# One shared-expert unit moved ahead of the block loop, routing of the last batches in other banks, and half of the last additions on GpSimd

## What is computed

```python
def reference(...):
    x = x + tanh(g_xattn[0]) * xattn(layernorm(x), ctx, ctx, mask, Wq, Wk, Wv, Wo, 16)
    h = layernorm(x)
    shared = (silu(h @ shared_gate.T) * (h @ shared_up.T)) @ shared_down.T
    probs = sigmoid(h @ router_w.T + routing_bias)
    scores, indices = top_k(probs, 2)            # scores divided by their sum
    g = silu(h @ gate_w[e]); u = h @ up_w[e]     # e: the two experts of the token
    combined = sum over the two of score * ((g * u) @ down_w[e])
    return x + tanh(g_ffn[0]) * (shared + combined)
```

## Time and profile before

| what | value |
|---|---|
| time, median of 3 runs | 181.72 us (181.02 to 184.23) |
| the profiled execution's own time | 181.07 us |
| its span, first to last instruction | 179.3 us |
| mean granted clock of PE | 0.993 of full |
| PE busy | 165.0 us, 92% |
| DVE busy | 126.9 us, 71% |
| POOL busy | 108.4 us, 60% |
| ACT busy | 109.3 us, 61% |

### The profile page before, as it was taken

One profiled execution on the slowest core, in us unless ns is written; L12 is line 12 of the kernel. 1 busy time (PEld: TensorE's weight loads), 2 busy tenths in 40 slices (PEclk: granted clock), 3 DMA queues, 4 the chain that ended last, 5 costly groups with the idle time before them and its releaser, 6 DMA issues.

```text
span 179.3 us, 4668 instructions
## 1 busy us (share of the span) xinstructions
PE 165.0 (92%) x1424; PEld 140.2 (78%) x1424; DVE 126.9 (71%) x613; ACT 109.3 (61%) x402; POOL 108.4 (60%) x137
## 2 busy tenths in 40 slices
PE   7899889999999999999999999988899999998960
PEld 7777669988889998779998779876586887886840
DVE  2779988756898766798776798778746666663364
ACT  3657997468588267598367698513546666663210
POOL 3666799846796816866706868686444666666200
PEclk9999999999999999999999999999999999999997
DMA  5999994900000000101000000013132222211063
GB/s 154 262 372 375 412 410 191 385 23 4 16 0 18 0 2 4 32 19 44 1 4 0 15 21 32 15 49 91 45 89 65 63 66 78 73 53 35 12 223 117
DMA packets 11095, 17.34 MB, mean 97 GB/s; under 512 B 2075, under 2 KB 6945, under 8 KB 10944
## 3 DMA queue, kind: packets, MB, share of 16 engines
q1 hardware_dynamic: 9504, 14.59, 24.0%
q0 software_dynamic: 1280, 2.20, 3.7%
q10 hardware_dynamic: 288, 0.26, 0.4%
HBM read 9.99 MB, written 7.51 MB: 98 GB/s over the span
## 4 chain that ended last, share of the span: by engine, by line
PE 62%; DVE 13%; ACT 8%; DMA 6%; POOL 5%; issue 4%; SPq 1%
PE misc L397 8%; PE pt L650 7%; PE s_even L360 6%; PE o_bank L386 6%; ACT probs L716 4%; PE pt L371 4%; PE proj_q L317 3%; DMA wq_raw<-wqT 3%; PE proj_k L317 3%; DVE probs L925 3%; PE proj_k L319 2%; PE pt L641 2%; PE proj_k L318 2%; PE proj_q L319 2%; PE proj_q L318 2%
## 5 line engine op out<-in xcount | busy, mean ns | idle before, releaser
L716 ACT ACTIVATE probs<-probs,negmax 128x128 f32<-128x128 f32 x128 | 50.0, 395 | 8.5 <-DVE negmax L925 8.5
L1311 POOL TENSOR_TENSOR probs<-probs,rinv 128x512 f32<-128x512 f32 x32 | 33.1, 1046 | 24.6 <-DVE rinv L939 24.3
L1420 POOL DMA_INDIRECT ys<-probsT,xg x23 | 22.5, 979 | 17.2 <-issue 10.7
L716 ACT ACTIVATION_READ_ACCUMULATOR probs<-probs,negmax 128x1 f32 x128 | 24.4, 191 | 0.0
L925 DVE CUSTOM_DVE_ANT_0 probs<-s_even,mask 128x128 f32<-128x128 f32 x64 | 18.1, 282 | 3.8 <-issue 3.8
L1341 POOL DMA_INDIRECT xs<-xrow,slot x16 | 16.3, 1019 | 6.5 <-issue 3.9
L371 PE MATMUL pt<-ident_sb,probs 128*128 128x128 f32 x128 | 17.6, 277 | 1.6 <-POOL probs L1311 1.1
L360 PE MATMUL s_odd<-kT,qT 64*128 64x128 f32 x128 | 18.5, 285 | 0.0
L360 PE MATMUL s_even<-kT,qT 64*128 64x128 f32 x128 | 18.5, 284 | 0.0
L925 DVE CUSTOM_DVE_ANT_0 probs<-s_odd,mask 128x128 f32<-128x128 f32 x64 | 18.1, 283 | 0.0
L650 PEld LDWEIGHTS pt<-down_sb,v 128*128 128x128 f32 x92 | 12.1, 190 | 7.2 <-issue 7.1
(11 more groups left out here) (279 smaller groups left out, 455.0 us busy)
## 6 DMA issues: line engine op xcount, KB each, us to landing
xs<-pad SPq DMA_DIRECT2D x5, 858.0 KB, 5.8
xg<-xs SPq DMA_DIRECT2D x23, 66.0 KB, 1.9
down_sb<-down SPq DMA_DIRECT2D x1, 1152.0 KB, 8.9
probs<-ys SPq DMA_DIRECT2D x4, 256.0 KB, 4.0
gu_raw<-gu SPq DMA_DIRECT2D x3, 256.0 KB, 6.5
wk_raw<-wkT SPq DMA_DIRECT2D x2, 256.0 KB, 3.8
wq_raw<-wqT SPq DMA_DIRECT2D x2, 256.0 KB, 5.0
mask<-mask SPq DMA_DIRECT2D x8, 64.0 KB, 2.0
```

The costliest lines, as they stand in the source:

```text
L716: e = act.activation(probs[:, r, l, :], probs[:, r, l, :], ACT.Exp, bias=negmax[:, r, l:l + 1], scale=-1.0, accum_out=rowsum[:, r, l:l + 1])
L1311: pool.tensor_tensor(quad, quad, rinv[:, r, 4 * u:4 * u + 4].unsqueeze(2).to_broadcast([P, 4, P]), ALU.mult).then_inc(norm_done, 1)
L1420: pool.indirect_dma_start(out=ys, out_offset=bass.IndirectOffsetOnAxis(ap=xg[n % IN_FLIGHT][:, P:P + 1].bitcast(U32), axis=0), in_=y_sb[n ...
```

## The change

Four things change. (1) PE works unit 0 of the shared expert ahead of the block loop, in place of the six fillers; unit 1 takes unit 0's place in the loop, and only units 2 and 3 are left behind it. ACT's and DVE's work on unit 0 moves to the first and second turn of the loop, that on unit 1 to the place where unit 0's was. (2) So that `proj_q` and `proj_k` are free for unit 0, routing rounds 3 and 4 (batches 6 and 7) use `pt0` and `pt1`. (3) POOL adds the first row of each pair into `x_sb`; DVE adds the second row after it, and the shared part last. (4) Pairs 0 and 1 are stored together once the first `add_shared` is done, pairs 2 and 3 together after the second. The banks of the units and of the down steps are renamed to match.

```diff
-        shared_banks = [(proj_bank["q"], proj_bank["k"]), (o_bank, misc), (s_bank[0], s_bank[1]), (proj_bank["q"], proj_bank["k"])]
-        d_bank = [pt_bank[0], proj_bank["q"]]
+        shared_banks = [(proj_bank["q"], proj_bank["k"]), (proj_bank["q"], proj_bank["k"]), (o_bank, misc), (s_bank[0], s_bank[1])]
+        d_bank = [proj_bank["k"], proj_bank["q"]]
-        route_bank = [misc, misc, proj_bank["q"], proj_bank["q"], proj_bank["k"]]
+        route_bank = [misc, misc, proj_bank["q"], pt_bank[0], pt_bank[1]]
...
-            engine.wait_ge(sum_ready, n + 1)
+            engine.wait_ge(acc_done, 1 + n // 2)
             engine.dma_start(out[:, tiles, :], x_sb[:, tiles, :]).then_inc(out_sem, 16)
...
                 if r == LAST:
-                    pe.wait_ge(k_free, PROJ_USES * PAIRS)
+                    pe.wait_ge(pt1_free, GROUPS)
+                elif r == 3:
+                    pe.wait_ge(pt0_free, GROUPS)
                 elif r:
                     pe.wait_ge(at_ready, r)
-                if r == 3:
-                    pe.wait_ge(counts_read, 1)
...
             experts = {n: block_expert(n) for n in range(2)}
-            stay_warm(6)
+            pe.wait_ge(counts_read, 1)
+            shared_pass(0, 0)
+            shared_pass(0, 1)
             x2_transposes(LAST)
...
                 if n + 2 == EARLY:
-                    pe.wait_ge(counts_read, 2)
-                    shared_pass(0, 0)
-                    shared_pass(0, 1)
+                    pe.wait_ge(h_done, 1)
+                    shared_pass(1, 0)
+                    shared_pass(1, 1)
...
             pe.wait_ge(xglo_ready, BLOCKS)
-            shared_pass(1, 0)
+            shared_pass(2, 0)
             block_down(BLOCKS - 1, experts[BLOCKS - 1])
-            shared_pass(1, 1)
-            pe.wait_ge(h_done, 1)
-            shared_pass(2, 0)
             shared_pass(2, 1)
-            down_step(0)
+            pe.wait_ge(hid_ready, BLOCKS)
             shared_pass(3, 0)
             shared_pass(3, 1)
+            down_step(0)
             down_step(1)
...
+                if n == 0:
+                    silu(0)
                 if n + 2 == EARLY:
-                    silu(0)
+                    silu(1)
             block_y(BLOCKS - 1)
-            for unit in range(1, 4):
+            for unit in range(2, 4):
                 silu(unit)
...
+                if n == 1:
+                    hidden(0)
                 run(last_table, 1)
                 if n + 1 < BLOCKS:
                     block_hidden(n + 1)
                 run(last_table, 1)
                 if n + 1 == EARLY:
-                    hidden(0)
+                    hidden(1)
             block_hidT(BLOCKS - 1)
-            for unit in range(1, 4):
+            for unit in range(2, 4):
                 hidden(unit)
-            add_shared(0)
-            for n in range(4):
-                tiles = slice(2 * n, 2 * n + 2)
-                if n == 2:
-                    add_shared(1)
-                dve.wait_ge(acc_done, 1 + n // 2)
-                dve.wait_ge(in_y[n], 16)
-                dve.tensor_tensor(x_sb[:, tiles, :], y_of[:, tiles, 0, :], x_sb[:, tiles, :], ALU.add).then_inc(first_added, 1)
-                dve.wait_ge(first_added, n + 1)
-                dve.tensor_tensor(x_sb[:, tiles, :], y_of[:, tiles, 1, :], x_sb[:, tiles, :], ALU.add).then_inc(sum_ready, 1)
+            for half in range(2):
+                for n in (2 * half, 2 * half + 1):
+                    tiles = slice(2 * n, 2 * n + 2)
+                    dve.wait_ge(first_added, n + 1)
+                    dve.tensor_tensor(x_sb[:, tiles, :], y_of[:, tiles, 1, :], x_sb[:, tiles, :], ALU.add).then_inc(second_added, 1)
+                dve.wait_ge(second_added, 2 * half + 2)
+                add_shared(half)
...
+            for n in range(4):
+                tiles = slice(2 * n, 2 * n + 2)
+                pool.wait_ge(in_y[n], 16)
+                pool.tensor_tensor(x_sb[:, tiles, :], y_of[:, tiles, 0, :], x_sb[:, tiles, :], ALU.add).then_inc(first_added, 1)
```

More of the change, by code:

```diff
@@ L209, in build @@
         th_done, hidT_ready, yb_done, y_ready = sem("th_done"), sem("hidT_ready"), sem("yb_done"), sem("y_ready")
-        first_added, sum_ready = sem("first_added"), sem("sum_ready")
+        first_added, second_added = sem("first_added"), sem("second_added")
         xs = nc.dram_tensor("xs", (SLOTS, WIDTH), F32).ap()
@@ L215, in build @@
         y_rows = probs.rearrange("p r l k -> p (r l) k")[:, 0:B * TOP_K, :]
+        y_of = y_rows.rearrange("p (b k) h -> p b k h", k=TOP_K)
         def load_y(engine, n):
@@ L1258, in _ @@
                 if n + 1 == EARLY:
-                    hidden(0)
+                    hidden(1)
             block_hidT(BLOCKS - 1)
-            for unit in range(1, 4):
+            for unit in range(2, 4):
                 hidden(unit)
-            add_shared(0)
-            y_of = y_rows.rearrange("p (b k) h -> p b k h", k=TOP_K)
-            for n in range(4):
-                tiles = slice(2 * n, 2 * n + 2)
-                if n == 2:
-                    add_shared(1)
-                dve.wait_ge(acc_done, 1 + n // 2)
-                dve.wait_ge(in_y[n], 16)
-                dve.tensor_tensor(x_sb[:, tiles, :], y_of[:, tiles, 0, :], x_sb[:, tiles, :], ALU.add).then_inc(first_added, 1)
-                dve.wait_ge(first_added, n + 1)
-                dve.tensor_tensor(x_sb[:, tiles, :], y_of[:, tiles, 1, :], x_sb[:, tiles, :], ALU.add).then_inc(sum_ready, 1)
+            for half in range(2):
[5 more added lines that the diff above has]
+                add_shared(half)
         @block.gpsimd
```

## The result

The changed kernel takes 182.26 us against 181.25 us before (medians of 20 runs each); the ratio is 1.0051, 95% interval 1.003 to 1.0072. Two of the changed kernel's runs, at 190.8 and 262.2 us with a granted clock of 0.85 and 0.57, are not in the ratio. So it is slower by 0.9 us, a real difference and far under 2%. The profiled execution took 182.20 us with a span of 180.2 us; 0.9 us more span than before, and 0.2 us more around it.

A forecast was written before the change was run, and what follows sets the result against it. PE bounds the block loop; behind it, last shared unit, silu, product, down step, then DVE, with the landing of `ys` next. From 181.07: 0 ahead, 0 in the loop, +0.5 additions, +0.2 stores: 181.8, range 180.4 to 183.2.

The forecast's parts named there:

- Ahead of the loop, price 0: Unit 0 replaces the fillers before the block loop and ends near 120.9; transposes wait for DVE anyway: 0, at worst 0.2 us.
- In the loop, price 0: First turns: DVE's early product pushes block 2's product, idle time and PE's shared pass absorb it: 0, without that cover 0.2.
- PE behind the loop gains 3 us: Second down step ends at 171.5 at most, against 174.48; no program gain, since rows of `ys` land from 172.5 to 174.2.
- the rival in which the end follows PE: Behind the loop, freed PE time is the bound and the end moves by up to 3.0 us, to 178; chance 0.03.
- The additions, +0.5: Behind the loop, POOL and DVE take turns on additions with both operands in SBUF: 0.5 us later; chance 0.5.
- the two orders: Contested turn behind the loop: POOL first, shared part ends 177.8, 0.7 later; DVE first, 177.45 to 177.85, 0.3 to 0.7 later.
- The rival without holding (-0.35): Behind the loop, POOL and DVE do not hold each other up: -0.35 + 0.2 for stores, 180.9; chance 0.25.
- the undisturbed case: Additions behind the loop without mutual holding: POOL works 172.6 to 175.5, DVE ends the shared part by 176.75; chance 0.25.
- The rival of a starved DVE: Behind the loop, POOL's four additions run through to 175.5, DVE's follow to 178.7, 1.6 later; 182.9 with stores; chance 0.12.
- The stores, +0.2: At the end, pairs 2 and 3 leave together instead of the last alone: 0.2 us, between 0 and 0.3.

The follow-up runs named there:

- the PE part alone: Changed kernel's work on PE, ACT and in the loop, with additions and stores as in the kernel before: 0.9956, on the quieter chip 0.9997 (181.01 us).
- the run through a bank: Changed kernel, but PE copies the second rows into free banks, so DVE's second-row additions read one operand from a bank: ratio 0.9995 to the kernel before.
- The pair-by-pair stores: Changed kernel, but the shared part is added pair by pair and each pair stored by itself: 0.9989, then 1.0026 (181.90 us) to the kernel before.
- the run with the shared parts first and POOL adding: Changed kernel, but DVE adds both shared parts before the rows of `ys` arrive and each pair is stored by itself: ratio 1.0028 to the kernel before.
- the kernel whose sums began at 172.79: Changed kernel, but shared parts first, PE sums both rows of every pair in a bank, DVE adds once a pair, POOL nothing: 0.9975 to the kernel before.

## Why the prediction was right

**Ahead of the loop, price 0: right.** The transposes came at 120.96, held by DVE as before. **In the loop, price 0: right in the sum, and partly by luck.** Block 2's product was pushed and the idle time before the copy took it up, as worked out. But the loop began 0.2 us early, by the second gather, and lost 0.3 at blocks 17 to 19, by a later one; neither was in the prediction, and they offset each other to the 0.1 us of the loads. The kernel before has one slower step there (1.69 us), the changed kernel run again has two like the first time, the PE part alone in its quiet run none. What makes that gather late in some kernels is not shown; on two other chips single steps of about 2.3 us and more turn up at other blocks.

**PE behind the loop gains 3 us, and they are worth nothing: right.** The second down step ended at 171.25 (said: 171.5 at most), and PE left the chain. The PE part alone, at 0.9956 and 0.9997, excludes the rival in which the end follows PE. One step of the reading was wrong without harm. The prediction has the end of the kernel before set by the last unit, its silu, its product, *its down step*, then DVE. The chain of waits of the kernel before goes past that down step:

```profile
171.69 0.69 DVE qT L1182
172.37 0.67 DVE x_sb L1188
...
173.07 0.43 DVE x_sb L1271
```

The down step ended at 174.48, but DVE was busy with pair 1 until 174.74. What PE's last unit held up was DVE's product, and with it the first shared part and the first row at 173.07, with the first rows there since 172.5. So no more than about 0.5 us was to be had from PE in that order from the start.

**The additions, +0.5: right in mechanism, the size helped by luck.** The last DVE instruction ended at 177.66; the two orders had given 177.8 and 177.45 to 177.85. The two engines took turns, in the first of the two orders, with DVE held for 0.5 us twice and POOL for 0.18 twice. For that order the prediction had 5.2 us from 172.6; it took 4.78, since the additions follow each other closer than their durations (POOL's second began 0.68 us after its first). And POOL started at 172.88 instead of 172.6, after a landing of 3.8 instead of 3.6 us. The two errors, 0.4 and 0.3 us, work against each other. The rival without holding (-0.35) is out by the trace, and the run through a bank shows the reason given to be the right one: the same additions on both engines, none stretched, and a row of 4.2 us without its wait for a load, where the undisturbed case had been worked out at 4.15 (172.6 to 176.75). The rival of a starved DVE is out too: POOL's third and fourth additions were held by DVE in turn. The Trainium skill ("SBUF — State Buffer", "Who interferes with whom") says that both operands in SBUF make the collision, and that whoever is issued first goes first; the traces agree with both (0.93 us held here, 0.42 through a bank; POOL's pair 2, issued at 174.24, goes ahead of DVE's pair 1, issued at 174.48). Its "whole instruction" is by these rows slightly too hard: POOL's pair 1 row ends at 174.28, and DVE's held addition, if it takes 0.42 us once it runs, began at 174.14. The rows can't tell whether POOL still reads in those last 0.14 us.

**The stores, +0.2: the mis-sized term.** The last store landed after 2.1 us, 0.4 over a lone one, where I had taken 0.2, and 0.3 as the most. The step was to halve what the loads of 256 KB showed; two stores of 128 KB issued in the same instant cost each other more. The pair-by-pair stores confirm the term: each lands in 1.7 us, and on the quieter chip that kernel is 0.6 us faster.

**Not in the sum: 0.2 us around the span.** The changed kernel's own time lies 2.0 us above its span, the kernel before 1.8. In the profiled executions, five of the other six runs in which POOL adds at the end show 2.0 to 2.1, the seven without 1.8 to 1.9, and every other execution on record repeats this (1.95 to 2.08 and 1.74 to 1.88). The exception, at 1.8, is the run with the shared parts first and POOL adding, whose span is the one that ends 1.6 us after its last store. Why is not settled. It is the rest of the difference between the 181.8 that was forecast and the 182.2 of the profiled run.

**What the prediction did not ask** is what the freed 3 us could be used for. They let the shared parts be added before `ys` arrives, and that takes 0.8 us out of the row of additions. The change put the shared part last, behind the rows, and so spent nothing of what it had won on PE.

## What to carry to other kernels

When work leaves an engine at the end of a program, look for the transfer that the last stage waits for: here it landed from 172.8 us on, so 3 us of PE time bought nothing until the additions that don't need the transfer were put ahead of it. Half of a row of short additions given to a slower engine is no half: POOL took 0.72 us where DVE takes 0.42, and with two operands in SBUF each they held each other up; reading one operand from a bank ended that, and even then the row was no shorter than DVE's alone (4.4 us, 4.2 without the wait for a load, against 4.05). Before an idle PE is given late work, price it at either clock, and from the landing of its own data.

## What the runs showed of the hardware that was not expected

- Two stores of 128 KB issued in the same instant from two queues landed in 1.9 and 2.1 us, a lone one in 1.7.
- PE's clock after idle time was not the same in two kernels. After 2.34 us of idleness and 1.16 us of work it fell to 0.50, and the next eight passes took 2.08 us. In the kernel whose sums began at 172.79, after 1.47 us of idleness, and went on without a gap, the clock stayed at 1.00 and eight passes took 1.06 to 1.16 us by the same view.
- A gather of 66 KB issued in the same half microsecond as a transfer of instructions landed in 2.6 us instead of 1.8 to 1.9 (2.2 to 2.7 in the other traces of the quieter chip with such a transfer). That the one causes the other is not shown.
